# Two of five count blocks of an attention unit multiplied on POOL, with factors made by ACT, while DVE reads its factors from PSUM

## The chip, the cores and the metric

One Trainium2 chip; the kernel runs on 1 core. The metric is the device time of one execution in microseconds (us), median over runs. One execution was also taken by the hardware profiler; its own time stands beside the runs below. PE is TensorE (the matrix engine), DVE is VectorE, ACT is ScalarE, POOL is GpSimd, and SP is the queue that issues most transfers here.

## The reference

A graph of 3125 nodes with 128 features and 103,125 edges goes through two layers, each with a residual and a normalisation. The first multiplies gathered rows by a filter of the edge and sums them by destination. The second, which the change concerns, is an attention over the same edges:

```python
h_att = features @ Watt_w + Watt_b
a1, a2 = (a[:d], a[d:])
e = jax.nn.leaky_relu(h_att[src] @ a1 + h_att[dst] @ a2, SLOPE)      # SLOPE = 0.2
e = e - jnp.max(e)
exp_e = jnp.exp(e)
denom = jax.ops.segment_sum(exp_e, dst, num_segments=num_nodes)
alpha = exp_e / (denom[dst] + 1e-09)
h_msg = features @ W1_w + W1_b
h_neigh = jax.ops.segment_sum(h_msg[src] * alpha, dst, num_segments=num_nodes)
...
return jax.nn.leaky_relu(sum_h + prod_h @ W2_w + W2_b, SLOPE)
```

## The kernel before

**First part (to about 1090 us).** The first layer: loops over the edges in groups, in which PE, ACT and DVE make the edge filter, POOL issues the scattered transfers, and counting matmuls fill a table c_tab in HBM: how many edges go from node s to node t. The change does not touch it. From there to 1160 us the late rows of the first layer are added, the first normalisation is done, and the scores and messages of the second layer are made.

**Attention by counts.** Since the weight of an edge depends on its two nodes only, the sum over edges is a matrix product. Sources are in 25 blocks of 128 (partitions), destinations in 25 blocks of 126. For source s with score s1 and destination t with score s2, exp(leaky_relu(s1 + s2)) is, up to common factors, s1_part times max(s1_gate, gates[t]): s1_gate is one number per source (a column per block), gates a row over destinations. The message rows in msg_sb are scaled by s1_part on ACT. The counts are multiplied by max(gates, s1_gate), which `weights(n)` does on DVE (L2692, one scalar_tensor_tensor per count block of 128 x 630, in place in c_in):

```python
nc.vector.scalar_tensor_tensor(counts_here,
                               gates[:, c * CQ:(c + 1) * CQ].rearrange("p (t n) -> p t n", n=Q),
                               s1_gate[:, h * HG + k:h * HG + k + 1], counts_here, ALU.max,
                               ALU.mult).then_inc(w_done, 1)
```

PE then sums the weighted counts against the messages (L2434: per count block five float32 products of 128 x 126 with 129 columns, shown as ten instructions).

**Units.** UNITS holds 25 pairs (c, h): chunk c of five destination blocks, and h, a group of HG = 5 source blocks. Units run c-outermost, so units 0 to 4 are chunk 0. The counts of a unit come with one transfer into one of CR = 4 buffers (`load_counts`, L2253, on SP), asked for once PE has finished the unit four before (a_used). All orders are written out by hand in the blocks of the engines, tied by semaphores.

**What DVE does between.** The guard 1e-9 in the denominator needs the largest score over existing edges. `masked_best(h)` (L2677, a custom DVE instruction and an accumulator read) takes, for source block h, the largest of mask times s2_b over 3150 destinations; the mask is uint8 and the scores are float32, both in SBUF. Two run before unit 0; BESTS sets how many follow each unit's weights: two after each of units 0 to 7, one after each of units 8 to 14. After unit 15 come `candidates`, `largest`, `guard_bias` and `guard`, short steps over PE and ACT; TOP_AT is 15 and FROM is 18. From unit 18 on chunks are finished: average and division (`average`, `divided`), transposition back (`turn_back`, L2371), mix (L2771, L2773), output products (L2381, L2385), slope and residual, second normalisation.

**ACT and POOL in this stage.** ACT makes s1_gate, s1_part (L2541, L2543), the gates of chunk 0 (L2456), scales the 25 message blocks (L2548), makes the gates of the other chunks, and then copies finished chunks out of PSUM (`keep`, L2461). POOL has nothing between the first normalisation and the second.

Of the kernel before, what the change touches and what calls it, by code (L numbers as in the profile page):

```python
# [11 lines left out]
ALU = mybir.AluOpType  # L12
ACT = mybir.ActivationFunctionType
AX = mybir.AxisListType.X

P = 128
# [76 lines left out]
def build(nc, a, out):  # L93
    ctx = ExitStack()
    with ctx:
# [3 lines left out]
        def sem(name):  # L99
            return ctx.enter_context(nc.semaphore(name))  # L100
# [1994 lines left out]
        with ExitStack() as nodes:  # L2095
# [19 lines left out]
            s1_all = tmp("s1_all", [1, 1])  # L2115
            gate_top = tmp("gate_top", [P, 1])
            s1_bias = tmp("s1_bias", [P, 1])
            s2_bias = tmp("s2_bias", [P, 1])
            part_bias = tmp("part_bias", [P, 1])
            eps_part = tmp("eps_part", [P, 1])  # L2120
# [16 lines left out]
            neigh = plot([P, CB, D])[0:Q]  # L2137
            prod = plot([P, CQ])
            total = plot([P, CQ])
            sloped = plot([P, CB, D])[0:Q]  # L2140
            steep = plot([P, CB, D])[0:Q]
            late_lo = tmp("late_lo", [P, 2, CB, LK + 1])
            late_one = mask_room[:, 0:8 * CB * (LK + 1) * P].bitcast(F32).rearrange("p (u t n) -> p u t n", u=2, n=P)
# [29 lines left out]
            gm = sem("gm")  # L2173
            linked_done = sem("linked_done")
            hop = sem("hop")
            parts_done = sem("parts_done")
# [4 lines left out]
            w_done = sem("w_done")  # L2181
            a_used = sem("a_used")
            raw_done = sem("raw_done")
            inv_done = sem("inv_done")
# [17 lines left out]
            MIX_LAST = max(MIX_AT)  # L2202
            ACT_DIVIDES, ACT_FIRST, ACT_LAST = 3, 2, 2
            GM_S1, GM_MAX, GM_EPS = 3, 12, 16

            def num(c, b, n):
                return ps_wh[0:Q, c % 2, b // 3, b % 3 * MR:b % 3 * MR + n]
# [69 lines left out]
            @block.gpsimd  # L2277
            def _(pool):
                pool.wait_ge(ended, 1)
                all_added(pool, NH)  # L2280
                nc.gpsimd.memset(ln_eps[:], EPS).then_inc(xt_zero, 1)
                nc.gpsimd.memset(x1_t[:, QN:NP], 0.0).then_inc(xt_zero, 1)
                pool.wait_ge(xt_zero, 2)
                for c in range(NC):
                    refined(pool, mv, c, stats_done, rough, refine, rstd_done, 0)
                for c in range(NC - 1):
                    refined(pool, mv2, c, stats_done, rough, refine, rstd_done, NC)

            @block.tensor
            def _(pe):  # L2290
# [68 lines left out]

                def score_columns():  # L2360
                    for t in range(NB):
                        mm = nc.tensor.matmul(ps_d[0:Q, 1, 256 + t:257 + t], x1_t[:, t * Q:(t + 1) * Q], wa2b[:, 0:1],
                                              start=True, stop=True)
                    mm.then_inc(hop, 1)

# [87 lines left out]
            @block.scalar  # L2453
            def _(act):
                def gate_chunk(c):
                    nc.scalar.activation(gates[:, c * CQ:(c + 1) * CQ], s2_b[:, c * CQ:(c + 1) * CQ], ACT.Exp,  # L2456
                                         bias=s2_bias[:, 0:1], scale=SLOPE - 1.0).then_inc(gates_done, 1)

                def keep(c):
                    act.wait_ge(a_used, (c + 1) * HB)  # L2460
# [10 lines left out]

                def slope(c):
                    act.wait_ge(y_mm, c + 1)
                    need(act, summed, 2 * c)
                    nc.scalar.activation(sloped[:, :, :], out_flat(c)[0:Q, 0:CB * P].rearrange("p (b d) -> p b d", d=D),
                                         ACT.Copy, scale=SLOPE).then_inc(slope_done, 1)
# [36 lines left out]
                for first, w in zip(firsts, LATE_BY_ACT):  # L2513
# [25 lines left out]
                act.wait_ge(gm, GM_S1 + 5)  # L2539
                act.wait_ge(msg_done, NC)  # L2540
                nc.scalar.activation(s1_gate[:], msg_sb[:, :, MR - 1], ACT.Exp, bias=s1_bias[:, 0:1],  # L2541
                                     scale=1.0 - SLOPE).then_inc(parts_done, 1)
                nc.scalar.activation(s1_part[:], msg_sb[:, :, MR - 1], ACT.Exp, bias=part_bias[:, 0:1],  # L2543
                                     scale=SLOPE).then_inc(parts_done, 1)
                gate_chunk(0)
                act.wait_ge(parts_done, 2)
                for b in range(NB):
                    nc.scalar.activation(msg_sb[:, b, 0:D + 1], msg_sb[:, b, 0:D + 1], ACT.Copy,  # L2548
                                         scale=s1_part[:, b:b + 1]).then_inc(msg_scaled, 1)
                for c in range(1, NC):  # L2550
                    gate_chunk(c)
                for c in range(KEPT):
                    keep(c)
                act.wait_ge(hop, 3)
                act.wait_ge(gm, GM_EPS)
                nc.scalar.activation(eps_raw[:], ps_d[0:Q, 1, 256:256 + NB], ACT.Exp, bias=eps_bias[0:Q, 0:1],
                                     scale=-1.0).then_inc(eps_made, 1)
# [19 lines left out]
            def _(dve):  # L2577
# [104 lines left out]
                def weights(n):  # L2682

                    c, h = UNITS[n]
                    if n == 0:
                        dve.wait_ge(parts_done, 1)
                    if h == 0:
                        dve.wait_ge(gates_done, c + 1)
# [187 lines left out]
```

## Time and profile before

| | |
|---|---|
| median of 3 runs | 1388.13 us (1387.00 to 1388.74) |
| profiled execution, its own time | 1386.31 us |
| its span in the profile | 1384.5 us |
| mean granted TensorE clock | 0.928 |
| busy over the span: PE, DVE, ACT, POOL | 84%, 87%, 62%, 59% |
| units 0 to 14 | 1162.3 to 1298.5 us |
| units 15 to 24 and the finish | 1298.5 to 1384.5 us |

The span is read from the first to the last instruction of the profile; the rest of the execution's own time lies around it. Busy shares are averages over stages of different kinds, so the stage of the units is read by itself.

### The profile page before, as it was taken

The numbers are of one execution on the slowest core, as the hardware profiler recorded it, in microseconds if no ns is written. First come the engines' busy times: TensorE is split into PE (matmuls) and PEld (weight loads), VectorE is DVE, ScalarE is ACT, GpSimd is POOL, SyncE is SP. The second block draws the span as 40 slices with busy tenths as digits, with TensorE's granted clock in tenths as the row PEclk, the third lists the DMA queues.
The fourth block names the chain that finished last, engine by engine and source line by source line (L and its number), as shares of the span: only waits on it lengthen the run. The fifth ranks groups of instructions, "written<-read, shape, count | busy, mean of one in ns | idle before, by whom it ended". The sixth has DMA issues, their size and how long they took to land. (4 is left out here: it accounts for less than half of the span.)

```text
span 1384.5 us, 27852 instructions
## 1 busy us (share of the span) xinstructions
PE 1156.9 (84%) x8980; PEld 940.2 (68%) x9072; DVE 1199.6 (87%) x2226; ACT 856.2 (62%) x2125; POOL 813.5 (59%) x905
## 2 busy tenths in 40 slices
PE   5786776799989868899979999999999495877895
PEld 4453454457778646788757887777777484877895
DVE  8798876649999869899879999999998579999986
ACT  2564575577878878788878888888876054000023
POOL 3377777777777777777777777777777320000011
PEclk9697898799999999999999999999999797889998
DMA  8232242266998477899698998998898883766661
GB/s 258 80 92 83 82 131 81 75 160 173 241 271 235 150 249 219 236 245 253 207 238 222 271 261 256 241 260 231 241 268 226 210 254 116 237 207 231 226 218 38
DMA packets 246566, 276.09 MB, mean 199 GB/s; under 512 B 35079, under 2 KB 194470, under 8 KB 243078
## 3 DMA queue, kind: packets, MB, share of 16 engines
q1 hardware_dynamic: 197762, 183.84, 45.1%
q0 software_dynamic: 25792, 53.29, 12.2%
q10 hardware_dynamic: 22852, 37.02, 11.9%
q8 instruction: 78, 1.28, 0.4%
q14 instruction: 82, 0.67, 0.2%
HBM read 162.85 MB, written 111.20 MB: 198 GB/s over the span
## 5 line engine op out<-in xcount | busy, mean ns | idle before, releaser
L1977 POOL DMA_INDIRECT edge_rows<-x_rows,pos x806 | 779.6, 967 | 252.8 <-issue 229.5
L1475 ACT ACTIVATE h_edge<-ps_wh,w_col 128x128 f32<-128x128 f32 x808 | 229.3, 367 | 105.4 <-PE ps_wh L1276 100.3
L1320 PEld LDWEIGHTS ps_d<-back_one,back 128*128 128x128 f32 x1914 | 231.6, 193 | 60.9 <-issue 57.2
L1320 PE MATMUL ps_d<-back_one,back 128*128 128x128 f32 x1914 | 240.7, 278 | 5.1 <-DVE agg_t L1794 4.6
L1283 PE MATMUL ps_wh<-wf,filt 128*128 128x128 f32 x1616 | 236.6, 292 | 0.8 <-DVE filt L1577 0.7
L1269 PE MATMUL ps_v<-f_t,wf 128*128 128x512 f32 x400 | 222.4, 639 | 0.0
L1581 DVE TENSOR_TENSOR x_rows<-ps_wh,h_edge 128x512 f32<-128x512 f32 x202 | 138.2, 684 | 89.8 <-DMA edge_rows<-x_rows,pos 50.1
L1283 PEld LDWEIGHTS ps_wh<-wf,filt 128*128 128x128 f32 x1616 | 207.3, 201 | 2.8 <-DVE filt L1577 2.8
L1112 PE MATMUL ps_wh<-yard 128*128 128x150 bf16 x1575 | 138.4, 233 | 59.8 <-DVE yard L1102 37.4
L2434 PE MATMUL ps_wh<-loan,yard 128*126 128x129 f32 x1250 | 155.9, 289 | 37.8 <-DVE yard L2692 29.9
L1112 PEld LDWEIGHTS ps_wh<-yard 128*128 128x128 bf16 x1575 | 109.0, 100 | 105.0 <-DVE yard L1102 81.2
L2434 PEld LDWEIGHTS ps_wh<-loan,yard 128*126 128x126 f32 x1250 | 152.3, 202 | 40.6 <-DVE yard L2692 19.5
L1609 DVE TENSOR_TENSOR back_one<-back_lo,ps_d 128x128 f32<-128x128 f32 (+6 forms) x277 | 169.2, 611 | 6.0
L2077 POOL TENSOR_TENSOR ln_var<-mv,ln_eps 126x5 f32<-126x5 f32 x9 | 2.3, 261 | 257.9 <-DVE mv L2059 257.9
L1577 DVE SCALAR_TENSOR_TENSOR filt<-ps_v,sp_log 128x512 f32<-128x512 f32 x202 | 137.8, 682 | 15.5 <-ACT sp_log L383 15.4
L1102 DVE TENSOR_TENSOR yard<-yard,ps_d 128x1350 bf16<-128x1350 bf16 x175 | 148.9, 851 | 0.0
L379 ACT ACTIVATE sp_abs<-ps_v 128x512 f32<-128x512 f32 x202 | 120.8, 598 | 29.9 <-issue 24.3
L383 ACT ACTIVATE sp_log<-sp_abs 128x512 f32<-128x512 f32 x202 | 127.3, 630 | 6.4
L381 ACT ACTIVATE sp_abs<-sp_abs 128x512 f32<-128x512 f32 x202 | 127.3, 630 | 6.4
L1097 DVE TENSOR_TENSOR yard<-yard,ps_d 128x1152 bf16<-128x1152 bf16 x175 | 131.0, 748 | 0.0
L1488 ACT ACTIVATE yard<-ps_wh 128x450 f32<-128x450 f32 x175 | 107.5, 614 | 32.8 <-PE ps_wh L1112 30.8
L1276 PE MATMUL ps_wh<-h_win,onehot_t 126*128 126x128 bf16 x808 | 81.2, 224 | 46.9 <-issue 20.7
(344 smaller groups left out, 1368.2 us busy)
## 6 DMA issues: line engine op xcount, KB each, us to landing
c_tab<-yard SPq DMA_DIRECT2D x25, 1575.0 KB
yard<-c_tab SPq DMA_DIRECT2D x25, 1575.0 KB, 6.6
dst_bc<-dst ACTq DMA_DIRECT2D x99, 252.0 KB
back<-edge_rows SPq DMA_DIRECT2D x42, 516.0 KB
edge_rows<-x_rows,pos POOLq DMA_INDIRECT x806
back<-edge_rows SPq DMA_DIRECT2D x48, 258.0 KB
m_tab<-yard SPq DMA_DIRECT2D x25, 393.8 KB
mask_room<-m_tab SPq DMA_DIRECT2D x5, 1968.8 KB, 12.7
```

Source lines behind the costliest of these rows:

```text
L1097: nc.vector.tensor_tensor(oh_lo[:, buf, :, :].rearrange("p g (n u) -> p g n u", u=2), lo2[:, at, :].unsqueeze(2).to_broadcast([P, GP, P // ...
L1102: return nc.vector.tensor_tensor(oh_key[:, buf, :, :].rearrange("p g (n u) -> p g n u", u=2), key2[:, at, :].unsqueeze(2).to_broadcast([P, ...
L1112: mm = nc.tensor.matmul(count_bank[:, b * KW:(b + 1) * KW], oh_lo[:, buf, b * KT + k, :], oh_key[:, buf, b * KT + k, :], start=k == 0, sto ...
L1269: return nc.tensor.matmul(ps_v[:, j, :], wf1[:], rows, start=True, stop=True)
L1283: mm = nc.tensor.matmul(ps_wh[:, j, 0, q * D:(q + 1) * D], filt[:, j, q * P:(q + 1) * P], wf2[:], start=False, stop=True, skip_group_check ...
L1320: mm = nc.tensor.matmul(acc(c), back_rows(n)[:, k0 + t, 0:D], back_one[:, m % 2, o + t, :], start=t == 0, stop=t == k1 - k0 - 1, skip_grou ...
L1475: copy = nc.scalar.activation(h_edge[:, j, q, :], ps_wh[:, bank, 1, q * D:(q + 1) * D], ACT.Copy, scale=w_col[:, t(q)])
L1577: return nc.vector.scalar_tensor_tensor(filt[:, j, :], ps_v[:, j, :], 0.0, sp_log[:, j, :], ALU.max, ALU.add)
L1581: return nc.vector.tensor_tensor(x_rows[:, r, :, 0:D], ps_wh[:, j, 0, :].rearrange("p (q d) -> p q d", d=D), h_edge[:, j, :, :], ALU.mult)
L1609: return nc.vector.tensor_tensor(out, lo.unsqueeze(2).to_broadcast([P, count, P]), numbers.unsqueeze(1).to_broadcast([P, count, P]), ALU.i ...
L1977: return pool.indirect_dma_start(table[s], bass.IndirectOffsetOnAxis(places_here, 0), rows, None)
L2434: mm = nc.tensor.matmul(num(c, b, D + 1), c_in[:, n % CR, b, k, :], msg_sb[:, h * HG + k, 0:D + 1], start=h == 0 and k == 0 and b % 3 == 0 ...
```

## The change

In units 0 to 19 (chunks 0 to 3) the last two of the five count blocks go to POOL, which multiplies the counts by a finished factor (L2317 of the changed kernel). ACT makes that factor in two steps, as relu(gates - s1_gate) + s1_gate, which is max(gates, s1_gate), from a copy of the chunk's gates in SBUF; the four places for factors are the unused part of gates and the room of `sloped`. For DVE, ACT writes the chunk's gates into PSUM (ps_d), and DVE reads them there. Chunk 4 stays as it was: five multiplies on DVE, gates in SBUF. POOL begins a unit when the masked bests ahead of that unit are done. PE waits for w_pool ahead of the fourth and fifth block. ACT scales the messages in five groups of five, between the factors of units 0 to 4, and copies chunks out between later factors. The score columns go to ps_v instead of ps_d.

```diff
+            s1_less = tmp("s1_less", [P, NB])
-            sloped = plot([P, CB, D])[0:Q]
+            slope_room = plot([P, CB * D])
+            sloped = slope_room[0:Q, :].rearrange("p (b d) -> p b d", d=D)
...
+            SHARED = (NC - 1) * HB
+            POOL_K = 2
+            LARGER = 4
+            def by_dve(n):
+                return HG - POOL_K if n < SHARED else HG
+            def gates_at(c):
+                return ps_d_flat[:, 0:CQ] if c < NC - 1 else gates[:, c * CQ:(c + 1) * CQ]
+            def larger_at(m):
+                if m % LARGER == 0:
+                    return slope_room[:, 0:CQ]
+                return gates[:, m % LARGER * CQ:(m % LARGER + 1) * CQ]
...
+                for n in range(SHARED):
+                    pool.wait_ge(c_here[n % CR], (n // CR + 1) * 16)
+                    pool.wait_ge(linked_done, min(NB, BESTS[n]))
+                    for k in range(POOL_K):
+                        m = n * POOL_K + k
+                        pool.wait_ge(larger_made, (2 * n + 1) * POOL_K + k + 1)
+                        counts_here = c_in[:, n % CR, :, by_dve(n) + k, :]
+                        nc.gpsimd.tensor_tensor(counts_here, larger_at(m).rearrange("p (t n) -> p t n", n=Q), counts_here,
+                                                ALU.mult).then_inc(w_pool, 1)
...
                     for k in range(HG):
-                        pe.wait_ge(w_done, n * HG + k + 1)
+                        if k < by_dve(n):
+                            pe.wait_ge(w_done, dve_before(n) + k + 1)
+                        else:
+                            pe.wait_ge(w_pool, n * POOL_K + k - by_dve(n) + 1)
...
                 def gate_chunk(c):
-                    nc.scalar.activation(gates[:, c * CQ:(c + 1) * CQ], s2_b[:, c * CQ:(c + 1) * CQ], ACT.Exp,
-                                         bias=s2_bias[:, 0:1], scale=SLOPE - 1.0).then_inc(gates_done, 1)
+                    if c < NC - 1:
+                        if c:
+                            act.wait_ge(w_done, dve_before(c * HB))
+                        nc.scalar.activation(gates[:, 0:CQ], s2_b[:, c * CQ:(c + 1) * CQ], ACT.Exp, bias=s2_bias[:, 0:1],
+                                             scale=SLOPE - 1.0)
+                    nc.scalar.activation(gates_at(c), s2_b[:, c * CQ:(c + 1) * CQ], ACT.Exp, bias=s2_bias[:, 0:1],
+                                         scale=SLOPE - 1.0).then_inc(gates_done, 1)
+                def larger(n):
+                    c, h = UNITS[n]
+                    act.wait_ge(gates_done, gates_count(c))
+                    for k in range(POOL_K):
+                        m, j = n * POOL_K + k, h * HG + by_dve(n) + k
+                        if m >= LARGER:
+                            act.wait_ge(w_pool, m - LARGER + 1)
+                        nc.scalar.activation(larger_at(m), gates[:, 0:CQ], ACT.Relu, bias=s1_less[:, j:j + 1],
+                                             scale=1.0).then_inc(larger_made, 1)
+                    for k in range(POOL_K):
+                        m, j = n * POOL_K + k, h * HG + by_dve(n) + k
+                        act.wait_ge(larger_made, 2 * n * POOL_K + k + 1)
+                        nc.scalar.activation(larger_at(m), larger_at(m), ACT.Identity, bias=s1_gate[:, j:j + 1],
+                                             scale=1.0).then_inc(larger_made, 1)
...
-                    for k in range(HG):
+                    for k in range(by_dve(n)):
                         counts_here = c_in[:, n % CR, :, k, :]
-                        nc.vector.scalar_tensor_tensor(counts_here,
-                                                       gates[:, c * CQ:(c + 1) * CQ].rearrange("p (t n) -> p t n", n=Q),
+                        nc.vector.scalar_tensor_tensor(counts_here, gates_at(c).rearrange("p (t n) -> p t n", n=Q),
```

DVE in unit 0 before: the weights (L2692) and the two masked bests (the custom instruction is listed as ISA), up to the first multiply of unit 1. The names are the tensors: yard holds the counts c_in, agg_t the masked row that is thrown away, loan the scores.

```order
L2692 SCALAR_TENSOR_TENSOR yard<-gates,s_gate,yard 128x5x126 [waits c_here0,gates_done,parts_done]
L2692 SCALAR_TENSOR_TENSOR yard<-gates,s_gate,yard 128x5x126 x4
L2677 ISA agg_t,best<-mask_room,loan 128x3150 [waits linked_done]
L2677 ISA best 128x1
L2677 ISA agg_t,best<-mask_room,loan 128x3150 [waits linked_done]
L2677 ISA best 128x1
L2692 SCALAR_TENSOR_TENSOR yard<-gates,s_gate,yard 128x5x126 [waits c_here1]
```

The same place now (lines have moved: L2756 is L2692, L2743 is L2677):

```order
L2756 SCALAR_TENSOR_TENSOR yard<-ps_d,s_gate,yard 128x5x126 [waits c_here0,gates_done]
L2756 SCALAR_TENSOR_TENSOR yard<-ps_d,s_gate,yard 128x5x126 x2
L2743 ISA agg_t,best<-mask_room,loan 128x3150 [waits linked_done]
L2743 ISA best 128x1
L2743 ISA agg_t,best<-mask_room,loan 128x3150 [waits linked_done]
L2743 ISA best 128x1
L2756 SCALAR_TENSOR_TENSOR yard<-ps_d,s_gate,yard 128x5x126 [waits c_here1]
```

Three multiplies are left and read ps_d; the order is otherwise as before, and no wait was added on DVE.

ACT from s1_gate (s_gate here) on, before:

```order
L2541 ACTIVATE s_gate<-loan,s_bias 128x25 [waits msg_done,gm]
L2543 ACTIVATE s_part<-loan,part_bias 128x25
L2456 ACTIVATE gates<-loan,s_bias 128x630
L2548 ACTIVATE loan<-loan,s_part 128x129 [waits parts_done]
L2548 ACTIVATE loan<-loan,s_part 128x129 x24
L2456 ACTIVATE gates<-loan,s_bias 128x630 x4
```

and now, up to the factors of unit 1:

```order
L2599 ACTIVATE s_gate<-loan,s_bias 128x25 [waits msg_done,gm]
L2601 ACTIVATE s_part<-loan,part_bias 128x25
L2604 ACTIVATE s_less<-s_gate 128x25 [waits gates_done]
L2495 ACTIVATE gates<-loan,s_bias 128x630
L2497 ACTIVATE ps_d<-loan,s_bias 128x630
L2497 ACTIVATE gates<-loan,s_bias 128x630
L2507 ACTIVATE yard<-gates,s_less 128x630 [waits gates_done]
L2507 ACTIVATE gates<-gates,s_less 128x630
L2512 ACTIVATE yard<-yard,s_gate 128x630 [waits larger_made]
L2512 ACTIVATE gates<-gates,s_gate 128x630 [waits larger_made]
L2615 ACTIVATE loan<-loan,s_part 128x129 x5
L2507 ACTIVATE gates<-gates,s_less 128x630 [waits gates_done]
```

The gates of chunk 0 are made twice (SBUF and PSUM), then those of chunk 4; the factors of unit 0 come ahead of the first five messages (loan), and those of unit 1 ahead of the next five.

POOL had nothing between the two normalisations. Now the last two steps of the first, then units 0, 1 and the start of 2:

```order
L2088 TENSOR_TENSOR ln_rstd<-ln_var,ln_rstd 126x5 [waits refine]
L2090 TENSOR_TENSOR ln_back<-ln_back,ln_rstd 126x5 [waits refine]
L2317 TENSOR_TENSOR yard<-yard 128x5x126 [waits larger_made,linked_done,c_here0]
L2317 TENSOR_TENSOR yard<-gates,yard 128x5x126 [waits larger_made]
L2317 TENSOR_TENSOR yard<-gates,yard 128x5x126 [waits larger_made,linked_done,c_here1]
L2317 TENSOR_TENSOR yard<-gates,yard 128x5x126 [waits larger_made]
L2317 TENSOR_TENSOR yard<-yard 128x5x126 [waits larger_made,linked_done,c_here2]
```

Each unit is two multiplies; the first waits for factor, masked bests and counts.

## Rows read from the trace of the kernel before

**Rows 1.** The chain that ended last, 1160 us to the end, by line.
```profile
by line: DVE agg_t L2677 33.3%; DVE yard L2692 24.9%; PE ps_wh L2434 24.8%; issue 4.7%; PE ps_d L2385 2.0%; PE ps_d L2381 2.0%; PE ps_v L2371 1.2%; ACT room L2495 1.1%; DVE st L2055 0.5%; DVE yard L2773 0.4%; DVE room L2783 0.4%; DVE yard L
```
**Rows 2.** Windows: us, busy (x) of PE, PEld, DVE, ACT, POOL, PEclk, DMA share, GB/s.
```profile
1162.00:1173.00 11.00, 7.40 (x50) 7.24 (x50) 11.00 (x12) 8.21 (x23) 0.00 (x0) 0.78 0.11 20
1183.60:1194.20 10.60, 8.66 (x50) 8.50 (x50) 10.60 (x10) 0.00 (x0) 0.00 (x0) 0.68 1.01 318
1247.50:1254.80 7.30, 6.37 (x42) 6.37 (x43) 7.30 (x10) 0.00 (x0) 0.00 (x0) 0.77 0.57 214
1276.70:1283.90 7.20, 5.77 (x50) 5.58 (x50) 7.20 (x8) 0.00 (x0) 0.00 (x0) 1.00 0.65 224
1299.50:1367.50 68.00, 67.88 (x609) 67.13 (x609) 57.60 (x117) 17.14 (x49) 8.97 (x21) 1.00 0.53 181
```
**Rows 3.** Timeline of DVE: start us, us, line, operation, count.
```profile
1162.32 4.01 DVE L2692 SCALAR_TENSOR_TENSOR yard<-gates,s_gate,yard 128x630 f32<-128x630 f32 x5
...
1183.61 0.08 DVE L2677 DVE_READ_ACCUMULATOR2_ANT best<- 128x1 f32 x1
1183.61 4.01 DVE L2692 SCALAR_TENSOR_TENSOR yard<-gates,s_gate,yard 128x630 f32<-128x630 f32 x5
1187.54 3.43 DVE L2677 CUSTOM_DVE_ANT_0 agg_t<-mask_room,loan 128x3150 bf16<-128x3150 uint8 x1
...
1247.51 4.01 DVE L2692 SCALAR_TENSOR_TENSOR yard<-gates,s_gate,yard 128x630 f32<-128x630 f32 x5
...
1298.52 4.01 DVE L2692 SCALAR_TENSOR_TENSOR yard<-gates,s_gate,yard 128x630 f32<-128x630 f32 x5
```
**Rows 4.** Timeline of PE: the sums of units 8 and 9, and of unit 15.
```profile
1248.43 13.06 PE L2434 MATMUL ps_wh<-loan,yard 128*126 128x129 f32 x100 [3.22 <-DVE yard L2692]
...
1299.54 5.74 PE L2434 MATMUL ps_wh<-loan,yard 128*126 128x129 f32 x50 [1.61 <-DVE yard L2692]
```
**Rows 5.** Groups of POOL's instructions, out<-in xcount | busy us, mean ns | idle before.
```profile
L624 POOL TENSOR_TENSOR h<-h_left,h 128x640 bf16<-128x640 f32 x4 | 5.6, 1396 | 19.4 <-ACT h L571 19.4
```
**Rows 6.** Timeline of DVE (two rows), then of POOL (two rows), near 1345 us.
```profile
1344.28 0.87 DVE L2773 SCALAR_TENSOR_TENSOR yard<-ps_v,b,room 128x630 f32<-128x630 f32 x1
1345.06 1.65 DVE L2692 SCALAR_TENSOR_TENSOR yard<-gates,s_gate,yard 128x630 f32<-128x630 f32 x2
...
1344.60 0.20 POOL L2084 TENSOR_TENSOR ln_var<-ln_var,ln_rstd 126x5 f32<-126x5 f32 x1
1345.16 0.82 POOL L2088 TENSOR_TENSOR ln_rstd<-ln_var,ln_rstd 126x5 f32<-126x5 f32 x1
```
**Rows 7.** Timeline of DVE (three rows), then of POOL (two rows), 25 to 34 us.
```profile
26.04 0.82 DVE L739 TENSOR_TENSOR h_sum<-ps_v,b_in_b 128x640 f32<-128x640 f32 x1
...
29.36 0.83 DVE L748 TENSOR_TENSOR h_left<-h_sum,h 128x640 f32<-128x640 f32 x1
...
31.88 1.23 DVE L748 TENSOR_TENSOR h_left<-h_sum,h 128x640 f32<-128x640 f32 x1 [0.89 <-DVE att_sum L841]
...
25.90 1.40 POOL L624 TENSOR_TENSOR h<-h_left,h 128x640 bf16<-128x640 f32 x1 [9.71 <-ACT h L571]
31.04 1.40 POOL L624 TENSOR_TENSOR h<-h_left,h 128x640 bf16<-128x640 f32 x1 [3.74 <-ACT h L571]
```
**Rows 8.** Timeline of ACT ahead of unit 0.
```profile
1158.76 0.34 ACT L2541 ACTIVATE s_gate<-loan,s_bias 128x25 f32<-128x25 f32 x1 [8.70 <-DVE s_bias L2806]
...
1159.94 7.42 ACT L2548 ACTIVATE loan<-loan,s_part 128x129 f32<-128x129 f32 x25
1167.27 2.94 ACT L2456 ACTIVATE gates<-loan,s_bias 128x630 f32<-128x630 f32 x4
```
**Rows 9.** Timeline of DVE, then of POOL: a result and the start that waits for it.
```profile
1343.22 0.45 DVE L2059 BATCH_NORM_AGGREGATE mv<-st 126x2 f32<-126x6 f32 x5
...
1343.74 0.19 POOL L2077 TENSOR_TENSOR ln_var<-mv,ln_eps 126x5 f32<-126x5 f32 x1 [5.55 <-DVE mv L2059]
```
**Rows 10.** DMA issues of the page: KB each, median us from issue to landing.
```profile
yard<-c_tab SPq DMA_DIRECT2D x25, 1575.0 KB, 6.6
```

More of the change, by code:

```diff
@@ L2175, in build @@
             hop = sem("hop")
-            parts_done = sem("parts_done")
             gates_done = sem("gates_done")
@@ L2181, in build @@
             w_done = sem("w_done")
+            w_pool = sem("w_pool")
+            larger_made = sem("larger_made")
             a_used = sem("a_used")
@@ L2204, in build, with dve_before, gates_count @@
             GM_S1, GM_MAX, GM_EPS = 3, 12, 16
+            SHARED = (NC - 1) * HB
[3 more added lines that the diff above has]
+                return HG - POOL_K if n < SHARED else HG
+            def dve_before(n):
+                return sum(by_dve(u) for u in range(n))
+            def gates_at(c):
+                return ps_d_flat[:, 0:CQ] if c < NC - 1 else gates[:, c * CQ:(c + 1) * CQ]
+            def gates_count(c):
+                return (4 if c == 0 else 5) + min(c, NC - 2)
+            def larger_at(m):
+                if m % LARGER == 0:
+                    return slope_room[:, 0:CQ]
+                return gates[:, m % LARGER * CQ:(m % LARGER + 1) * CQ]
             def num(c, b, n):
@@ L2361, in score_columns @@
                     for t in range(NB):
-                        mm = nc.tensor.matmul(ps_d[0:Q, 1, 256 + t:257 + t], x1_t[:, t * Q:(t + 1) * Q], wa2b[:, 0:1],
+                        mm = nc.tensor.matmul(ps_v[0:Q, 1, 256 + t:257 + t], x1_t[:, t * Q:(t + 1) * Q], wa2b[:, 0:1],
                                               start=True, stop=True)
@@ L2473, in slope @@
                     act.wait_ge(y_mm, c + 1)
+                    if c == 0:
+                        act.wait_ge(w_pool, SHARED * POOL_K)
                     need(act, summed, 2 * c)
@@ L2541, in _ @@
                 nc.scalar.activation(s1_gate[:], msg_sb[:, :, MR - 1], ACT.Exp, bias=s1_bias[:, 0:1],
-                                     scale=1.0 - SLOPE).then_inc(parts_done, 1)
+                                     scale=1.0 - SLOPE).then_inc(gates_done, 1)
                 nc.scalar.activation(s1_part[:], msg_sb[:, :, MR - 1], ACT.Exp, bias=part_bias[:, 0:1],
-                                     scale=SLOPE).then_inc(parts_done, 1)
+                                     scale=SLOPE).then_inc(gates_done, 1)
+                act.wait_ge(gates_done, 1)
+                nc.scalar.activation(s1_less[:], s1_gate[:], ACT.Copy, scale=-1.0).then_inc(gates_done, 1)
                 gate_chunk(0)
[L2546 to L2557, printed above, removed]
+                gate_chunk(NC - 1)
+                act.wait_ge(gates_done, 2)
+                for n in range(SHARED):
+                    c, h = UNITS[n]
+                    if c and h == 0:
+                        gate_chunk(c)
+                    larger(n)
+                    if c == 0:
+                        for b in range(h * HG, (h + 1) * HG):
+                            nc.scalar.activation(msg_sb[:, b, 0:D + 1], msg_sb[:, b, 0:D + 1], ACT.Copy,
+                                                 scale=s1_part[:, b:b + 1]).then_inc(msg_scaled, 1)
+                    elif h == 1:
+                        keep(c - 1)
+                    if n == FROM:
+                        act.wait_ge(hop, 3)
+                        act.wait_ge(gm, GM_EPS)
+                        nc.scalar.activation(eps_raw[:], ps_v[0:Q, 1, 256:256 + NB], ACT.Exp, bias=eps_bias[0:Q, 0:1],
+                                             scale=-1.0).then_inc(eps_made, 1)
                 for n in range(FROM, len(UNITS)):
@@ L2684, in weights @@
                     c, h = UNITS[n]
-                    if n == 0:
-                        dve.wait_ge(parts_done, 1)
                     if h == 0:
-                        dve.wait_ge(gates_done, c + 1)
+                        dve.wait_ge(gates_done, gates_count(c))
                     dve.wait_ge(c_here[n % CR], (n // CR + 1) * 16)
-                    for k in range(HG):
+                    for k in range(by_dve(n)):
                         counts_here = c_in[:, n % CR, :, k, :]
-                        nc.vector.scalar_tensor_tensor(counts_here,
-                                                       gates[:, c * CQ:(c + 1) * CQ].rearrange("p (t n) -> p t n", n=Q),
+                        nc.vector.scalar_tensor_tensor(counts_here, gates_at(c).rearrange("p (t n) -> p t n", n=Q),
                                                        s1_gate[:, h * HG + k:h * HG + k + 1], counts_here, ALU.max,
```

## Prediction

> **What bounds the kernel now.** I read the chain that ended last first. From 1160 us on, two DVE lines (L2677, the masked best, and L2692, the weighting of the counts) hold 58% of it and PE's sums over the counts (L2434) 25% [rows 1]. Then I split that stretch by units [rows 2]: in the windows of single units DVE is busy all of the time and PE is not, whatever clock it has; from 1299.5 to 1367.5 us PE is busy all of the time. Last, I read DVE's own order [rows 3]. A unit is five multiplies of 0.786 us (3.93 us), then two masked bests (6.72 us) or one (3.36 us). Units 0 to 7 have two: from 1162.32 to 1247.51 us that is 10.65 us each. Units 8 to 14 have one: up to 1298.52 us, 7.29 us each. PE starts unit 15 at 1299.54 us and has no gap worth the name from there to 1367.5 us [rows 2, 4]. So a microsecond taken from DVE in units 0 to 14 moves the end by a microsecond, and one taken later moves nothing, since PE is in front there. The rest of the program (before 1160 us) is untouched.
>
> **What leaves DVE.** Two of five multiplies in each of 20 units. In units 0 to 14 that is 2 x 0.786 = 1.57 us a unit, 15 x 1.57 = 23.6 us. In units 15 to 19 it is worth nothing, because PE bounds them. The multiplies that stay read their factor from PSUM. The nearest row is L2773, the same operation and size with one input in PSUM: 0.78 us from its start to the next [rows 6], so I leave the price at 0.786 us; its recorded 0.87 us would be the upper end, and is covered by POOL's time below.
>
> **What POOL adds, and why DVE pays for part of it.** The nearest row to a multiply of 128x630 is the subtraction of 128x640 at L624: 1.40 us [rows 5]; I take 1.40 for each. It has one output type and contiguous operands, the new one runs in place over five pieces of 126, so I keep 1.30 and 1.65 us as ends. The question is what the two engines do to each other, and the trace has both directions. POOL behind DVE: POOL's small operation of 0.20 us stays 0.20 beside L2773 (one input in PSUM), and takes 0.82, to the end of the DVE instruction, beside L2692 (both inputs in SBUF) [rows 6]. DVE behind POOL: L748, two inputs in SBUF, takes 0.83 us alone and 1.23 when it meets POOL's L624; it starts at 31.88 and ends as if it had begun at 32.30, 0.14 us before POOL's end. L739, with one input in PSUM, takes 0.82 beside the same POOL operation [rows 7]. So an instruction with two SBUF inputs and a POOL operation exclude each other for whole instructions, and one with a PSUM input passes. The weighting thus passes after the change. The masked best reads mask and scores, both in SBUF, and I expect it to exclude POOL.
>
> The Trainium skill, "SBUF — State Buffer", section "Who interferes with whom", says so too: a DVE instruction with two SBUF inputs contends with a GpSimd instruction that reads SBUF, and the second to issue waits for all of the first. By that rule the sum is the one below; a saving of the full 23.6 us would be what remains without it.
>
> **The new unit.** POOL waits for the masked bests ahead of the unit, so both engines start together. POOL starts 0.07 us after what it waits for ends [rows 9], and that is the accumulator read, which ends 0.08 us into DVE's first multiply [rows 3]: 0.15. Two multiplies end at 2.95, and DVE may go at 2.81 (0.14 earlier, as above). DVE's three multiplies end at 2.36, so its masked best waits 0.45 us. The unit is 2.81 + 6.72 = 9.53 or 2.81 + 3.36 = 6.17 us, 1.12 us less than before in either kind. Units 1 to 14: 14 x 1.12 = 15.7 us.
>
> **Unit 0** pays for ACT's new work. Before, ACT made the factors of unit 0 with one exponential and then scaled the messages [rows 8]. An ACT instruction of 128x630 costs 0.71 us from start to start (four in 2.94 us, the last 0.81). Now: s1_gate at 1158.76, s1_part, s1_less to 1159.5, three exponentials from there (PSUM copy done at 1161.0, before DVE needs it at 1162.32), two Relu to 1163.0, two Identity that end at 1163.8 and 1164.5. POOL then works until 1166.7 and the masked best, ready at 1164.68, starts at 1166.56: 1.9 us of waiting against 1.57 saved, a loss of 0.3. Should DVE get between the two POOL multiplies, the second waits for the next gap and the sum is the same. The first five messages are scaled at 1166.0 instead of 1161.5, so PE starts about 2.7 us later; with 7.4 us it ends near 1173.5, when DVE is at unit 1: hidden by PE's idle time, 11.00 - 7.40 = 3.6 us in that window [rows 2].
>
> **What costs nothing, and its cover.** ACT's four instructions a unit are 2.9 us, under 6.17; if they were late POOL would be. They come after a chunk's exponentials only in units 5, 10 and 15: from DVE's last use of the old chunk on, two exponentials (1.5 us), two Relu (1.4) and the first Identity (0.8) make 3.7, against the 3.8 us (0.45 + 3.36) until DVE starts the unit. No wait, and nothing to spare. PE needs POOL's blocks as fourth and fifth of five, at about 4.4 us after DVE starts; they are there at 1.5 and 2.95. The counts land 6.6 us after issue [rows 10] and are asked for as soon as PE frees one of four buffers, three units (18 us) ahead. In PE's stretch the score columns go to another bank at the same price, and ACT's factors of unit 19 (2.9 us) stand ahead of its first division, which has a whole unit of PE as its cover.
>
> **PE as the next limit.** At full clock a unit takes it 5.74 to 5.77 us, 0.4 under the new 6.17. The granted clock was 0.68 in the window of 8.66 us, still under 9.53; it was 0.77 in unit 8 and 1.00 in unit 12 [rows 2]. Units 8 and 9 took 13.06 us together [rows 4], 0.7 over two new units; at 0.4 a unit this is caught up by unit 11. So nothing is lost at unit 15.
>
> **Sum.** 15.7 - 0.3 = 15.4 us. From the profiled execution, 1386.3 us, this gives 1370.9; the median of the runs shown is 1.8 us above that execution, so I predict 1388.1 - 15.4 = 1372.7 us. POOL's ends move it by 2 x 15 us for each microsecond: 1.30 gives 3.0 less (1369.7), 1.65 gives 7.5 more (1380.2).
>
> **Rivals.** (A) The masked best does not exclude POOL. It is a custom instruction of which no row stands beside POOL work. Then units 0 to 7 take 2.36 + 6.72 = 9.08 (8 x 1.57 = 12.6 us saved) and units 8 to 14 are PE's 5.74 (7 x 1.55 = 10.9): 23.4 us, less up to 1.6 for PE's two slow units, 1364.7 to 1366.3. For it: the operation is new to the evidence; against: it has both inputs in SBUF, as L2692 and L748 have. Chance 0.14. The Trainium skill, same page and section, says that on this chip a tensor_reduce never contends; if the custom one counted as such, this rival would be the outcome, though its second input speaks for the other sentence.
> (B) PE keeps a low clock in the denser units 8 to 14. At 0.77 (5.74 / 0.77 = 7.45 us) PE would bound them: units 1 to 7 save 7.8, unit 0 loses 0.3, units 8 to 14 lose 7 x 0.16 = 1.1, and 6.4 us saved give 1381.7. Against: the clock is 1.00 in unit 12 with PE busy four fifths of it, and the new units keep PE busier. Chance 0.04.
> (C) Slower. The weighting still reads its counts through what POOL needs and excludes it after all. Then three multiplies and POOL's two follow one another: 2.36 + 2.80 = 5.16 against 3.93, +1.23 a unit, 15 x 1.23 = 18.5, 1406.6. It decides as soon as POOL's two multiplies hold DVE up for more than the 1.57 us saved per unit; a POOL multiply above 1.96 us (half of 3.93, the old length of the weighting) would do the same by its length alone. Against: the 0.20 and 0.82 us rows above. For: POOL there handled 5 elements, not 630. Chance 0.08.
> (D) No change: POOL's multiply near 1.9 us, so that wait and saving cancel, 1388. Chance 0.04.
>
> **Numbers.** The forecast (1368 to 1381, with POOL's price free between its ends) has 0.70, A 0.14, B 0.04, C 0.08, D 0.04. The range reaches from A to the upper end of POOL's price and B: 1364 to 1381, and leaves out C, D and half of B. A measurement of this kernel can tell about 0.2% (2.8 us) from no change: faster 0.88, same 0.04, slower 0.08.
>
> **What would show it.** DVE: three multiplies of 0.79 us reading ps_d per unit, and the first masked best of a unit recorded long, 3.8 us instead of 3.43 (the wait lies inside its record); later ones 3.43. Period 9.5, then 6.2 us, and the start of unit 15 near 1283. POOL: forty operations of 1.40 us that begin 0.15 us after DVE's. PE without a gap from unit 15 on, for the same 68 us. All masked bests at 3.43 would be A; multiplies by DVE above 0.9 us or POOL's stretched by them C; a low clock and PE gapless in units 8 to 14 B. Any wait of PE on POOL that ends last would be a step I have at nothing.

## The result: 1376.8 us against 1387.0, and the profile after

| | before | after |
|---|---|---|
| median, first comparison (5 runs each) | 1387.00 us | 1376.80 us (1371.59 to 1378.16) |
| ratio, 95% interval | | 0.9916 (0.9898 to 0.9934) |
| median, second comparison (11 and 6 runs) | 1388.30 us | 1375.43 us (1372.81 to 1378.22) |
| ratio, 95% interval | | 0.9910 (0.9895 to 0.9925) |
| profiled execution, its span | 1386.31, 1384.5 us | 1371.59, 1369.6 us |
| DVE starts unit 0, unit 15 | 1162.32, 1298.52 us | 1160.40, 1283.38 us |
| units 0 to 14 | 136.20 us | 122.98 us |
| unit 15 to the end of the span | 85.98 us | 86.22 us |

The changed kernel is faster, by 10.2 us between the medians of the first comparison and 12.9 of the second; 15.4 were forecast (1372.7 us, range 1364 to 1381). The two profiled spans differ by 14.9 us, but 1.9 of that lies ahead of unit 0, in code that the change leaves alone. In the stages that it touches, DVE's (units 0 to 14) gains 13.2 us and the rest loses 0.2: 13.0 us together.

DVE's timeline of the changed kernel (start us, us, line and operation; L2756 is the weighting, L2743 the masked best):

```profile
1160.40 2.43 DVE L2756 SCALAR_TENSOR_TENSOR yard<-ps_d,s_gate,yard 128x630 f32<-128x630 f32 x3
1162.75 4.03 DVE L2743 CUSTOM_DVE_ANT_0 agg_t<-mask_room,loan 128x3150 bf16<-128x3150 uint8 x1
...
1166.70 4.53 DVE L2743 CUSTOM_DVE_ANT_0 agg_t<-mask_room,loan 128x3150 bf16<-128x3150 uint8 x1
...
1171.16 2.43 DVE L2756 SCALAR_TENSOR_TENSOR yard<-ps_d,s_gate,yard 128x630 f32<-128x630 f32 x3
1173.51 4.17 DVE L2743 CUSTOM_DVE_ANT_0 agg_t<-mask_room,loan 128x3150 bf16<-128x3150 uint8 x1
...
1177.61 3.43 DVE L2743 CUSTOM_DVE_ANT_0 agg_t<-mask_room,loan 128x3150 bf16<-128x3150 uint8 x1
...
1180.97 2.42 DVE L2756 SCALAR_TENSOR_TENSOR yard<-ps_d,s_gate,yard 128x630 f32<-128x630 f32 x3
1183.32 3.94 DVE L2743 CUSTOM_DVE_ANT_0 agg_t<-mask_room,loan 128x3150 bf16<-128x3150 uint8 x1
...
1239.13 2.42 DVE L2756 SCALAR_TENSOR_TENSOR yard<-ps_d,s_gate,yard 128x630 f32<-128x630 f32 x3
...
1245.35 2.42 DVE L2756 SCALAR_TENSOR_TENSOR yard<-ps_d,s_gate,yard 128x630 f32<-128x630 f32 x3
...
1283.38 2.42 DVE L2756 SCALAR_TENSOR_TENSOR yard<-ps_d,s_gate,yard 128x630 f32<-128x630 f32 x3
1285.72 0.92 DVE L2762 TENSOR_SCALAR none_low<-best 128x25 f32<-128x25 f32 x1
1286.56 1.59 DVE L2763 SCALAR_TENSOR_TENSOR raised<-best,low_less,loan 128x25 f32<-128x25 f32 x1
1288.19 1.21 DVE L2765 TENSOR_TENSOR cand<-raised,none_low 128x25 f32<-128x25 f32 x1
```

They answer to [rows 3]. The weighting is three instructions in 2.35 us (start to start), at the price of before. From unit 1 on, the first masked best of a unit is recorded as 4.17 or 3.94 us, in turn, the second as 3.43: the first contains a wait of 0.74 or 0.51 us. Units with two bests last 9.81 and 9.58 us, with one (from 1239.13 on) 6.22 and 6.46.

POOL's timeline beside it:

```profile
1161.95 1.52 POOL L2317 TENSOR_TENSOR yard<-yard 128x630 f32<-128x630 f32 x1 [21.90 <-ACT yard L2512]
1163.43 4.50 POOL L2317 TENSOR_TENSOR yard<-gates,yard 128x630 f32<-128x630 f32 x1
1171.37 3.01 POOL L2317 TENSOR_TENSOR yard<-gates,yard 128x630 f32<-128x630 f32 x2 [3.44 <-DVE best L2743]
1181.18 1.52 POOL L2317 TENSOR_TENSOR yard<-yard 128x630 f32<-128x630 f32 x1 [6.80 <-issue]
1182.66 1.30 POOL L2317 TENSOR_TENSOR yard<-gates,yard 128x630 f32<-128x630 f32 x1
```

POOL starts 0.21 us after DVE's first multiply (1180.97 and 1181.18). In unit 2 its two end at 1183.96, and the masked best that took 3.94 us behaves as if begun at 1183.83, 0.13 before. In unit 0 the second multiply shows 4.50 us: DVE's masked best came between, and only then POOL had its turn.

DVE's last three rows are small steps to the guard, behind the multiplies of unit 15. Before, they took 0.17, 0.26 and 0.19 us; here POOL's multiplies of units 15 and 16 stand beside them, and they take 0.92, 1.59 and 1.21. So DVE begins unit 16 late, and PE, which waits for its first block, starts that unit 6.19 us after unit 15 (1284.38 to 1290.57) instead of 5.98. That is the 0.2 us lost behind unit 15.

PE's timeline, and ACT's ahead of unit 0:

```profile
1164.02 14.02 PE L2470 MATMUL ps_wh<-loan,yard 128*126 128x129 f32 x100 [10.57 <-ACT loan L2615]
...
1240.05 18.51 PE L2470 MATMUL ps_wh<-loan,yard 128*126 128x129 f32 x150 [2.37 <-DVE yard L2756]
...
1265.41 5.77 PE L2470 MATMUL ps_wh<-loan,yard 128*126 128x129 f32 x50 [0.69 <-DVE yard L2756]
...
1284.38 5.74 PE L2470 MATMUL ps_wh<-loan,yard 128*126 128x129 f32 x50 [0.54 <-DVE yard L2756]
...
1290.57 5.77 PE L2470 MATMUL ps_wh<-loan,yard 128*126 128x129 f32 x50
```

```profile
1160.98 0.81 ACT L2512 ACTIVATE yard<-yard,s_gate 128x630 f32<-128x630 f32 x1
1161.69 0.81 ACT L2512 ACTIVATE gates<-gates,s_gate 128x630 f32<-128x630 f32 x1
1162.40 1.56 ACT L2615 ACTIVATE loan<-loan,s_part 128x129 f32<-128x129 f32 x5
```

PE still idles 0.4 to 0.7 us ahead of each of units 11 to 14, and from 1284.38 us on, but for those 0.2 us, it is as dense as before; the 14.02 us for units 0 and 1 are hidden. ACT's first factor is finished at 1161.79 and POOL starts at 1161.95.

### The profile page after: what moved, and what is told of

It reads as the page before. It is cut to its first block and busy times, and to the rows that moved or that the text cites. A ratio compares the mean times of both kernels' runs of the same rounds, so it can differ in the third digit from the quotient of the medians.

```text
span 1369.6 us, 27977 instructions
## 1 busy us (share of the span) xinstructions
PE 1155.7 (84%) x8980; PEld 938.9 (69%) x9072; DVE 1182.4 (86%) x2186; ACT 917.4 (67%) x2210; POOL 873.8 (64%) x945
## 5 line engine op out<-in xcount | busy, mean ns | idle before, releaser
L1283 PE MATMUL ps_wh<-wf,filt 128*128 128x128 f32 x1616 | 233.5, 289 | 0.6 <-DVE filt L1577 0.5
L1283 PEld LDWEIGHTS ps_wh<-wf,filt 128*128 128x128 f32 x1616 | 204.1, 198 | 2.6 <-DVE filt L1577 2.6
L1276 PEld LDWEIGHTS ps_wh<-h_win,onehot_t 126*128 126x128 bf16 x808 | 62.8, 99 | 72.1 <-issue 50.0
## 6 DMA issues: line engine op xcount, KB each, us to landing
mask_room<-m_tab SPq DMA_DIRECT2D x5, 1968.8 KB, 12.9
```

The costliest lines, as they stand in the source:

```text
L1276: mm = nc.tensor.matmul(ps_wh[:, bank, 1, q * D:(q + 1) * D], onehot_t[:, j, q * P:(q + 1) * P], rows, start=first_window and q == 0, stop ...
L1283: mm = nc.tensor.matmul(ps_wh[:, j, 0, q * D:(q + 1) * D], filt[:, j, q * P:(q + 1) * P], wf2[:], start=False, stop=True, skip_group_check ...
```

## The experiments

Besides medians I compare the time from DVE's start of unit 0 to its start of unit 15 in the profiled execution, which the noise ahead of unit 0 does not enter. It is 136.20 us before and 122.98 after.

**The same kernel again.**

> The changed kernel once more, since its five runs lay between 1371.6 and 1378.2 us while those of before lay within 3.5 us. Theory P: in some executions PE is granted a low clock in units 8 to 14, where the new unit of 6.2 to 6.5 us leaves it only 0.5 to 0.7 us beside 5.77 us of work; such an execution shows PE without idle time there and PE behind DVE when unit 15 starts, while DVE still takes 123 us from unit 0 to unit 15. Rival F: the difference lies before unit 0 (its start moves by 5 us), and the stage of units takes the same time. Rival L: DVE itself takes longer than 123 us from unit 0 to 15, because POOL and DVE meet otherwise. Times from 1371 to 1378 us again.

Measured: 1375.43 us (six runs, 1372.81 to 1378.22). DVE's and PE's rows of its profile:

```profile
1284.61 2.42 DVE L2756 SCALAR_TENSOR_TENSOR yard<-ps_d,s_gate,yard 128x630 f32<-128x630 f32 x3
```

```profile
1241.27 18.50 PE L2470 MATMUL ps_wh<-loan,yard 128*126 128x129 f32 x150 [2.53 <-DVE yard L2756]
...
1266.63 5.77 PE L2470 MATMUL ps_wh<-loan,yard 128*126 128x129 f32 x50 [0.69 <-DVE yard L2756]
...
1285.61 5.74 PE L2470 MATMUL ps_wh<-loan,yard 128*126 128x129 f32 x50 [0.53 <-DVE yard L2756]
```

Unit 0 starts at 1161.62 us, so the stage takes 122.99 us, the same as in the first profile, and PE has the same gaps at its end. The kernel before spreads too: 1385.57 to 1390.64 us over its 11 runs here. Over all profiled executions of this study unit 0 starts anywhere from 1160.40 to 1164.28 us with the same instructions ahead of it. Rival F thus accounts for up to 3.9 us between executions, and the two profiles speak against L. Neither was one of the long executions, so P is not refuted by them; it is merely not seen. F is not shown for the long ones either: with the stages as profiled, the run of 1378.22 us would need unit 0 to start near 1167 us, later than in any profile. But so would the longest run of the kernel before (1390.64 us), in which PE has some 1.5 us of idle time ahead of each of units 10 to 14; a spread of this size needs no P.

**DVE's factors from SBUF.**

```diff
-nc.vector.scalar_tensor_tensor(counts_here, gates_at(c).rearrange(...), ...
+nc.vector.scalar_tensor_tensor(counts_here, (gates[:, 0:CQ] if c < NC - 1 else gates_at(c)).rearrange(...), ...
```

> DVE reads its destination factors from the SBUF copy of the gates instead of PSUM; all else as in the changed kernel. Theory (two SBUF inputs exclude POOL for whole instructions): DVE's three multiplies and POOL's two no longer run beside each other, a unit is 2.36 + 2.82 to 3.02 + 6.72 = 11.9 to 12.1 us with two masked bests and 8.6 with one, 2.2 more than in the changed kernel: 15 x 2.2 = 33 us, about 1408 us, slower than the kernel before. Rival (the place of the gates does not matter, DVE's counts go the same way anyhow): multiplies of 0.79 us on DVE, no change, about 1375 us.

Measured: 1407.45 us (1406.45 to 1407.83), ratio to before 1.0136 (1.0120 to 1.0151). DVE, then POOL, in unit 2:

```profile
1186.99 4.74 DVE L2756 SCALAR_TENSOR_TENSOR yard<-gates,s_gate,yard 128x630 f32<-128x630 f32 x3
1191.66 3.43 DVE L2743 CUSTOM_DVE_ANT_0 agg_t<-mask_room,loan 128x3150 bf16<-128x3150 uint8 x1
...
1195.02 3.43 DVE L2743 CUSTOM_DVE_ANT_0 agg_t<-mask_room,loan 128x3150 bf16<-128x3150 uint8 x1
```

```profile
1187.20 2.04 POOL L2317 TENSOR_TENSOR yard<-yard 128x630 f32<-128x630 f32 x1 [7.52 <-issue]
1189.20 1.87 POOL L2317 TENSOR_TENSOR yard<-gates,yard 128x630 f32<-128x630 f32 x1
```

Three multiplies take 4.67 us from start to start instead of 2.35 (one by one they are recorded as 0.86, 2.12 and 1.91), POOL's are stretched to 2.04 and 1.87, and from unit 1 on the masked best waits for nothing any more: the two engines take turns at each instruction. Units 0 to 14 take 148.98 us, 26.0 more than with PSUM, and the change would have been a loss. The unit is 11.39 us (11.61 in odd ones) where I had said 11.9 to 12.1: POOL's pair adds 2.32 us to DVE's three, not the full 2.8, as the turns overlap a little at their ends. The total of 1408 us was right only by luck: 26.0 us came in units 0 to 14 where I had 33, and another 6.5 behind unit 15, which I had not counted: PE idles there seven times for 0.5 to 1.5 us, mostly until DVE's late weights come, and the three small steps to the guard take 1.50, 1.37 and 1.43 us. The theory's mechanism holds: without the copy in PSUM the change loses 19 us against the kernel before, with it it gains 13.

**One block instead of two on POOL.**

```diff
-            POOL_K = 2
+            POOL_K = 1
```

> POOL gets one of five blocks instead of two (DVE four). Theory: POOL's 1.5 us end inside DVE's 4 x 0.786 = 3.14 us, so every masked best is back at 3.43 us and a unit takes 3.14 + 6.72 = 9.86 or 3.14 + 3.36 = 6.50 us, 0.15 more than the 9.70 and 6.33 of the changed kernel: 2.3 us more than its fast executions, about 1374. By theory P the slack of PE grows to 0.7 us a unit and the spread over executions becomes smaller, within 3 us. Rival (POOL work costs DVE something even beside instructions with a PSUM input, so that less POOL work is better): faster than the changed kernel.

Measured: 1375.22 us (1374.94 to 1378.03), stage 124.17 us.

```profile
1202.59 3.21 DVE L2756 SCALAR_TENSOR_TENSOR yard<-ps_d,s_gate,yard 128x630 f32<-128x630 f32 x4
1205.72 3.43 DVE L2743 CUSTOM_DVE_ANT_0 agg_t<-mask_room,loan 128x3150 bf16<-128x3150 uint8 x1
```

```profile
1183.11 1.52 POOL L2317 TENSOR_TENSOR yard<-gates,yard 128x630 f32<-128x630 f32 x1 [8.31 <-DVE best L2743]
...
1202.80 1.29 POOL L2317 TENSOR_TENSOR yard<-yard 128x630 f32<-128x630 f32 x1 [8.32 <-issue]
```

The masked best is back at 3.43 (3.42 to 3.43 in all 23), since POOL's one multiply ends inside DVE's four. The stage is 1.2 us longer than with two blocks (I had 2.3), since the second block's saving of 0.79 a unit is mostly paid back as waiting. Between medians nothing can be told apart. The first block brings 12.0 of the 13.2 us. Four of the five runs lie within 0.4 us and one is 3 us away, so the spread settles nothing on P. The small steps to the guard, which here have no POOL work beside them, are back at 0.17, 0.26 and 0.19 us, and the time behind unit 15 at 86.07.

**The places of two factors exchanged.** The profile held something that I had not expected: POOL's multiply takes 1.52 us in three cases and 1.30 in one, the second of even units.

```diff
-                if m % LARGER == 0:
+                if m % LARGER == 1:
                     return slope_room[:, 0:CQ]
-                return gates[:, m % LARGER * CQ:(m % LARGER + 1) * CQ]
+                at = (1, 0, 2, 3)[m % LARGER]
+                return gates[:, at * CQ:(at + 1) * CQ]
```

> Only the places of ACT's factors are exchanged: the factors of first multiplies of even units lie in the second fifth of gates and those of their second multiplies in the room of sloped. In the changed kernel POOL's multiply took 1.30 us for the second of an even unit and 1.50 to 1.52 for the three others. If the place of the factor decides, 1.30 moves to the first multiply of even units; if the place of the counts decides, it stays at the second. Time as the changed kernel (1371 to 1378 us) in both cases, since the sum of the two is the same.

Measured: 1375.03 us (1373.32 to 1377.83), stage 122.98 us. POOL in unit 2:

```profile
1182.89 1.53 POOL L2318 TENSOR_TENSOR yard<-gates,yard 128x630 f32<-128x630 f32 x1 [6.80 <-issue]
1184.38 1.30 POOL L2318 TENSOR_TENSOR yard<-yard 128x630 f32<-128x630 f32 x1
```

The short one stays second, now with its factor in yard, so the factor's place alone does not decide. Nor does the counts' place: in the run with one block per unit above, the same block (the fifth of an even unit) took 1.29 us in unit 4 and 1.52 in unit 2, where the factor lay elsewhere. What fits all of them is the difference between the two. Counted from the starts of yard and of gates, a block of counts and a factor begin at a byte offset of 0 or 8 within 16; each of their five pieces (504 bytes in the factor, 2520 in the counts) shifts both by 8. Equal offsets go with 1.52, unequal with 1.30.

**Places chosen so that all offsets differ.**

```diff
-                    return slope_room[:, 0:CQ]
-                return gates[:, m % LARGER * CQ:(m % LARGER + 1) * CQ]
+                    return slope_room[:, 2:2 + CQ]
+                at = (0, 1, 3, 2)[m % LARGER]
+                return gates[:, at * CQ:(at + 1) * CQ]
```

> POOL's multiply took 1.29 to 1.30 us in some cases and 1.52 in the others. In all 40 of the changed kernel and of the runs that moved its operands so far, the short ones are those whose factor and counts start at different offsets within 16 bytes (0 and 8), the long ones those where both are equal. Here only the places of the factors are chosen so that all differ (third and fourth fifth of gates exchanged, the room of sloped begun two elements later). Theory: every multiply 1.30 us, the first masked best of a unit about 3.7 us instead of 3.94 and 4.17, a unit 9.35 and 6.00 instead of 9.70 and 6.33: 15 x 0.34 = 5 us less than the changed kernel, 1370.5. Rival (the price follows the block or the place alone): the mix of 1.30 and 1.52 stays, and so does the time.

Measured: 1369.16 us (1368.65 to 1370.62), ratio to before 0.9863 (0.9847 to 0.9880), stage 118.22 us.

```profile
1182.35 2.43 DVE L2757 SCALAR_TENSOR_TENSOR yard<-ps_d,s_gate,yard 128x630 f32<-128x630 f32 x3
1184.70 3.72 DVE L2744 CUSTOM_DVE_ANT_0 agg_t<-mask_room,loan 128x3150 bf16<-128x3150 uint8 x1
...
1188.35 3.43 DVE L2744 CUSTOM_DVE_ANT_0 agg_t<-mask_room,loan 128x3150 bf16<-128x3150 uint8 x1
```

```profile
1182.56 1.30 POOL L2318 TENSOR_TENSOR yard<-yard 128x630 f32<-128x630 f32 x1 [6.80 <-issue]
1183.82 1.30 POOL L2318 TENSOR_TENSOR yard<-gates,yard 128x630 f32<-128x630 f32 x1
```

All of POOL's multiplies took 1.30 us, but for the one that waits for a masked best in unit 0; the wait in DVE's first masked best is 0.29, and the unit 9.36 (with one best 6.00, but 6.20 in unit 10, where ACT's first factor of the new chunk comes 0.2 us late). The stage is 4.8 us shorter (5 expected). Two elements of padding and an exchange of two places thus give a third as much again as the whole change did. It also bears on P: with units of 6.0 us PE has less slack than in the changed kernel (it idles 0.23 us ahead of units 12 to 14, not 0.4 to 0.7), and still the four runs lie within 2.0 us.

**ACT's gates of chunk 4 behind the factors of unit 0.**

```diff
-                gate_chunk(NC - 1)
                 act.wait_ge(gates_done, 2)
...
                     larger(n)
+                    if n == 0:
+                        gate_chunk(NC - 1)
```

> The former with ACT's gates of chunk 4 moved behind the factors of unit 0. Theory: POOL's first multiply starts 0.7 us earlier, and DVE waits 0.7 us less in unit 0: 1369.8. Rival (unit 0 is hidden by something else, ACT or PE): the same time as without the move.

Measured: 1368.69 us (1368.12 to 1369.08), ratio to before 0.9857 (0.9840 to 0.9873), stage 117.83 us.

```profile
1162.61 2.43 DVE L2758 SCALAR_TENSOR_TENSOR yard<-ps_d,s_gate,yard 128x630 f32<-128x630 f32 x3
1164.96 4.52 DVE L2745 CUSTOM_DVE_ANT_0 agg_t<-mask_room,loan 128x3150 bf16<-128x3150 uint8 x1
...
1169.41 3.43 DVE L2745 CUSTOM_DVE_ANT_0 agg_t<-mask_room,loan 128x3150 bf16<-128x3150 uint8 x1
```

Unit 0 is 10.16 us instead of 10.54: 0.4 gained of the 0.7 expected. DVE now waits once for both multiplies (4.52) where it waited twice. The medians do not separate it from the former; it has the lowest of all.

**POOL without its wait for the masked bests.**

```diff
-                    pool.wait_ge(linked_done, min(NB, BESTS[n]))
```

> POOL no longer waits for the masked bests ahead of a unit; it starts when counts and factors are there. Theory (exclusion for whole instructions, so what counts is how much of POOL's time lies beside DVE's PSUM multiplies): POOL's multiplies move to the borders between masked bests, where each costs DVE 1.3 to 1.5 us in full: up to 15 x 2.8 - 15 x 0.6 = 33 us more, 1388 to 1408; less if POOL's first one still falls beside the three multiplies. Rival (only the total of POOL's work and masked bests counts, wherever it lies): within 3 us of the changed kernel.

Measured: 1377.46 us (1375.24 to 1377.72), stage 124.98 us, 2.0 more than the changed kernel.

```profile
1181.18 4.74 DVE L2742 CUSTOM_DVE_ANT_0 agg_t<-mask_room,loan 128x3150 bf16<-128x3150 uint8 x1
...
1191.80 4.75 DVE L2742 CUSTOM_DVE_ANT_0 agg_t<-mask_room,loan 128x3150 bf16<-128x3150 uint8 x1
...
1249.28 3.42 DVE L2742 CUSTOM_DVE_ANT_0 agg_t<-mask_room,loan 128x3150 bf16<-128x3150 uint8 x1
```

```profile
1167.28 10.67 POOL L2316 TENSOR_TENSOR yard<-gates,yard 128x630 f32<-128x630 f32 x3
1177.91 4.71 POOL L2316 TENSOR_TENSOR yard<-yard 128x630 f32<-128x630 f32 x1
```

POOL asks too early, stands behind a masked best (4.71 us for a multiply), and where it gets in between two of them the second is recorded as 4.74: 1.31 us of DVE's time for one multiply, nearly all of its length. But this happens to few of the 23. A multiply that waited behind the last best of a unit runs beside the weights, and costs nothing. Adding up what the 23 masked bests of the stage take beyond 3.43 us gives 12.5 us here and 10.4 in the changed kernel: the 2.0. My theory's size was wrong by far, the rival is nearer; the mechanism is visible, and the wait is worth 2 us, not up to 33. The medians alone could not tell that.

**A fifth of POOL's second block back to DVE.**

```diff
+                        t = CB if k == 0 else CB - 1
-                        counts_here = c_in[:, n % CR, :, by_dve(n) + k, :]
+                        counts_here = c_in[:, n % CR, 0:t, by_dve(n) + k, :]
...
+                    if n < SHARED:
+                        counts_here = c_in[:, n % CR, CB - 1, HG - 1, :]
+                        nc.vector.scalar_tensor_tensor(counts_here, gates_at(c)[:, (CB - 1) * Q:CB * Q],
+                                                       s1_gate[:, h * HG + HG - 1:h * HG + HG], counts_here, ALU.max,
+                                                       ALU.mult).then_inc(w_done, 1)
```

> One of the five pieces of POOL's second block goes back to DVE (a fourth DVE instruction of 128x126 in the shared units). Theory: POOL's time falls by a fifth of 1.3 to 1.5 us (0.28), DVE's three multiplies become 2.36 + 0.2 = 2.56, still under POOL's 2.7: a unit 0.27 us shorter, 15 x 0.27 = 4 us less than the changed kernel, 1371.5. Rival (DVE's path, not POOL's, sets the unit): 15 x 0.2 = 3 us more, 1378.

Measured: 1370.94 us (1370.32 to 1371.69), stage 119.68 us, 3.3 less than the changed kernel.

```profile
1184.11 2.42 DVE L2760 SCALAR_TENSOR_TENSOR yard<-ps_d,s_gate,yard 128x630 f32<-128x630 f32 x3
1186.45 0.33 DVE L2765 SCALAR_TENSOR_TENSOR yard<-ps_d,s_gate,yard 128x126 f32<-128x126 f32 x1
1186.71 3.46 DVE L2747 CUSTOM_DVE_ANT_0 agg_t<-mask_room,loan 128x3150 bf16<-128x3150 uint8 x1
...
1190.10 3.43 DVE L2747 CUSTOM_DVE_ANT_0 agg_t<-mask_room,loan 128x3150 bf16<-128x3150 uint8 x1
```

The piece costs DVE 0.26 us, and the wait in an even unit is down to 0.03. So POOL's end, not DVE's own multiplies, set the unit in the changed kernel. The equal offsets of the operands were left as they are. With unequal ones POOL's two would end at about 2.55 us of the unit (0.21 + 1.30 + four fifths of 1.30) and DVE's four at 2.60, so little should be left for this edit to take; that is an estimate, and the two edits were not run together.

## Why the prediction was right, point by point

**The bound.** Right. DVE sets units 0 to 14, PE the rest: 13.2 us were gained in the first and nothing in the second (86.22 against 85.98 us).

**What leaves DVE.** Right. Reading PSUM costs DVE nothing here: three in 2.35 us, 0.78 each.

**Exclusion.** Right in both directions, and shown by taking its condition away: with both inputs in SBUF the same three multiplies take 4.67 us. The masked best, the one operation of which no row of before spoke, excludes POOL too: 0.51 and 0.74 us of waiting in each unit's first, none in the second (unit 0 apart), none with one block on POOL. That is what the Trainium skill says in "SBUF — State Buffer", section "Who interferes with whom"; its sentence on tensor_reduce, rival A, does not cover this custom instruction. So rivals A and C are both answered by rows, and not only by the time. The prediction looked at two kinds of DVE instruction only. A third kind takes turns too: L2762, a TENSOR_SCALAR with a single input in SBUF, took 0.92 us against 0.17 alone and ended 0.04 us after POOL's multiply.

**The size: where 15.4 became 13.0.** Three terms were off. (1) The step "I take 1.40 for each": a pair of multiplies is 2.78 us in even units, as I had it, and 3.01 in odd ones, 0.10 more on average; I had looked for the price in the operation and its length, and it also lies in the offsets of its operands. (2) POOL starts 0.21 us after DVE, not 0.15, and DVE is let in 0.13 us before POOL's end, not 0.14. Together 0.17 a unit, 14 x 0.17 = 2.4 us: units 1 to 14 gave 125.56 - 112.22 = 13.3 us where I had 15.7. (3) Unit 0 lasts 10.76 us, a loss of 0.1 instead of 0.3. Behind unit 15 come 0.2 us that I had at nothing: the guard's small steps taking turns with POOL. In sum 15.4 - 2.4 + 0.2 - 0.2 = 13.0 us.

**The cover of ACT's work.** Right, and as tight as said: in units 5 and 10 POOL starts 0.21 us after DVE as everywhere else, and once the units were shorter (6.00 us) ACT came 0.2 us late in unit 10.

**PE as next limit.** Right in what was profiled: 18.51 us for units 8 to 10 against 18.91 of DVE, and idle time again from unit 11 on. Rival B (a low clock in units 8 to 14) was not met.

**Between 13.0 and the 10.2 of the first medians** lies the spread of executions (the second medians gave 12.9). Of it, 3.9 us in where unit 0 starts are shown; whether a long execution loses anything inside the stage stays open, since no long one was profiled.

## What to carry to other kernels

Before work is moved from DVE to POOL, look at what each DVE instruction beside it reads. In these runs one with an input in PSUM ran beside POOL, and one with both in SBUF took turns with it, as did one small step with a single input in SBUF. A copy of one operand to PSUM by an engine with time to spare can decide between gain and loss (here 31 to 32 us). Where the engines take turns, POOL's work is free only as far as it lies beside DVE instructions that let it pass; line up the starts, and then size the share of POOL so that it ends with them. And read the durations of equal instructions one by one: two prices for one operation are a lead.

## What the runs showed of the hardware that was not expected

POOL's multiply of two float32 operands of 128x630, in place on the second, takes 1.29 to 1.31 us when their offsets within 16 bytes differ (0 and 8) and 1.51 to 1.54 when they are equal, wherever it does not wait for DVE. Three kernels that placed them differently agree, and the one in which all were made to differ got 1.30 throughout. Only offsets of 0 and 8 were tried, counted from the starts of the two tensors; why equal ones cost more was not looked into. Second, where POOL's operation waited behind a masked best and DVE's next masked best behind POOL's, the two alternated, one instruction each, in unit 0 of the changed kernel and where POOL's wait was taken out. Third, short DVE steps pay most: of 128x25 elements and 0.17 to 0.26 us alone, three of them took 3.7 us together beside POOL's multiplies.
